# Node-graph layer on one core: two tiles of x ahead of the node types, and the type scan in steps of the key pass

## What is computed

```python
xn = layernorm(x)                                     # per node, no gain
# 1. graph attention: per-type projections of xn, one softmax per edge type over all its edges
K, Q, V = (type_proj(xn, node_type, W, b) for W, b in (Wk, bk), (Wq, bq), (Wv, bv))
scores = sum((K[src] @ Wa[t]) * Q[dst]) / sqrt(32) * relation_pri[t]
agg = segment_sum(softmax(scores over edges of type t) * (V[src] @ Wm[t]), dst)
gnn = layernorm(agg + xn) * ln_g + ln_b
# 2. linear attention over all nodes
q, k, v = split(xn @ Wqkv.T);  q, k = elu(q) + 1, elu(k) + 1
kv, ksum = sum_s k[s] (x) v[s], sum_s k[s]            # a sum over all nodes
t = (q @ kv) / (q . ksum + 1e-6)
x1 = layernorm(t + xn) * g1 + b1;  mix = layernorm(mlp(x1) + x1) * g2 + b2
x = x + gnn + mix
# 3. feed-forward on the top half of the nodes by a routing weight, added to x
```

## Time and profile before

| | us |
|---|---|
| median of 3 runs | 1085.01 |
| lowest, highest | 1084.25, 1085.23 |
| profiled execution, its own time | 1085.92 |
| its span (first to last instruction) | 1083.9 |
| granted PE clock, mean over the span | 0.898 of full speed |

### The profile page before, as it was taken

One profiled execution on the slowest core, in us unless ns is written; L12 is line 12 of the kernel. 1 busy time (PEld: TensorE's weight loads), 2 busy tenths in 40 slices (PEclk: granted clock), 3 DMA queues, 4 the chain that ended last, 5 costly groups with the idle time before them and its releaser, 6 DMA issues. The chain is left out here.

```text
span 1083.9 us, 18408 instructions
## 1 busy us (share of the span) xinstructions
PE 911.0 (84%) x5317; PEld 652.2 (60%) x5317; DVE 803.5 (74%) x1700; ACT 589.0 (54%) x1532; POOL 637.6 (59%) x820
## 2 busy tenths in 40 slices
PE   4989999999848778778777878787769939999997
PEld 3776777777524444444444444444439828888886
DVE  6754788787648878888888888888858938885541
ACT  2655999988336666666666666666641203332121
POOL 4614777777577777777777777777720037662000
PEclk9999999999967888888888888888888969999999
DMA  9822343334477777787877777877717232210020
GB/s 284 245 77 89 124 167 134 142 137 139 166 238 231 239 238 235 238 235 237 236 238 240 235 236 237 236 236 239 228 57 255 86 106 79 59 35 5 1 97 22
DMA packets 96936, 183.09 MB, mean 169 GB/s; under 512 B 15845, under 2 KB 65580, under 8 KB 96836
## 3 DMA queue, kind: packets, MB, share of 16 engines
q0 software_dynamic: 38896, 129.86, 38.7%
q1 hardware_dynamic: 54660, 48.76, 14.9%
q10 hardware_dynamic: 3280, 3.28, 0.9%
HBM read 147.79 MB, written 34.06 MB: 168 GB/s over the span
## 5 line engine op out<-in xcount | busy, mean ns | idle before, releaser
L1356 POOL DMA_INDIRECT big<-kv_scratch,src_i x336 | 318.6, 948 | 102.3 <-issue 100.8
L1518 PE MATMUL ps<-edge 64*128 64x256 f32 x784 | 146.6, 505 | 4.1 <-DMA edge<-q_scratch 4.0
L1637 DVE TENSOR_TENSOR big<-big,ps 128x1024 f32<-128x1024 f32 x84 | 102.3, 1218 | 54.1 <-DMA big<-kv_scratch,src_i 53.9
L1534 PE MATMUL ps<-big,edge 128*64 128x256 f32 x672 | 116.7, 478 | 25.8 <-DVE big L1696 14.3
L1518 PEld LDWEIGHTS ps<-edge 64*128 64x128 f32 x784 | 86.7, 239 | 48.1 <-issue 34.6
L1421 ACT ACTIVATE edge<-edge 128x64 f32<-128x64 f32 x392 | 102.9, 334 | 0.0
L1644 DVE TENSOR_REDUCE ps<-big 128x32 f32<-128x1024 f32 x84 | 102.4, 1219 | 0.1
L1696 DVE TENSOR_TENSOR big<-big,ps 128x1024 f32<-128x1024 f32 x84 | 99.0, 1212 | 0.0
L1534 PEld LDWEIGHTS ps<-big,edge 128*64 128x64 f32 x672 | 53.1, 166 | 71.3 <-DVE big L1696 34.6
L2095 PE MATMUL ps<-big 128*128 128x256 f32 (+1 forms) x416 | 92.0, 377 | 2.2 <-ACT big L2013 2.2
L2026 ACT ACTIVATE big<-ps,fb 128x256 f32<-128x256 f32 (+1 forms) x104 | 39.5, 463 | 94.4 <-PE ps L2095 94.4
(11 more groups left out here) (346 smaller groups left out, 1965.3 us busy)
## 6 DMA issues: line engine op xcount, KB each, us to landing
edge<-q_scratch SPq DMA_DIRECT2D x196, 64.0 KB
big<-kv_scratch,src_i POOLq DMA_INDIRECT x336, 3.9
agg_scratch<-big SPq DMA_DIRECT2D x16, 252.0 KB
xn_scratch<-big ACTq DMA_DIRECT2D x5, 640.0 KB, 5.2
mix_scratch<-big SPq DMA_DIRECT2D x25, 128.0 KB, 1.7
edge<-mix_scratch SPq DMA_DIRECT2D x1, 3200.0 KB, 13.3
big<-xn_scratch SPq DMA_DIRECT2D x25, 128.0 KB, 2.6
edge<-in_x SPq DMA_DIRECT2D x24, 128.0 KB, 2.3
```

The costliest lines, as they stand in the source:

```text
L1356: pool.indirect_dma_start(kv_slots[s][:, k, :], None, kv_d[0:N, :], bass.IndirectOffsetOnAxis(ap=src_i[:, e:e + 1], axis=0)).then_inc(got[ ...
L1518: ins = pe.matmul(qr_ps[g % 2][:, (2 * hg + k) * D:(2 * hg + k + 1) * D], ohT[64 * hg:64 * hg + 64, g % 2, k * P:(k + 1) * P], qwin[64 * h ...
L1534: ins = pe.matmul(sums_of(g)[64 * hg:64 * hg + 64, :], oneh[:, s, k, hg * 64:hg * 64 + 64], kv_slots[s][:, 2 * hg + k, D:2 * D], start=(k ...
L1637: dve.tensor_tensor(k_rows, k_rows, qr_ps[g % 2].rearrange("p (k d) -> p k d", d=D), ALU.mult).then_inc(pr, 1)
```

## The change

Nothing is computed differently. The order and the place of steps in the prologue change:

- SP issues x tiles 0 and 1 and the key weights first, without waiting for a clearing; then types and the rest of x. The last x tile waits for a second clearing.
- POOL clears the types' tile first, makes the constants, and clears the raw edge tile and the last x row behind them. Its inverse deviations of parts 0 and 1 stand between the constants.
- There are six parts instead of four: tiles 0-1, 2-4, 5-9, 10-14, 15-19, 20-24.
- DVE takes statistics of tiles 0 and 1 first, then casts and marks the types, normalises tiles 0 and 1, takes the statistics of tiles 2 to 4, copies the type sums, and enters the key pass. The scan stands behind kf of tile 4, the first tiles behind 5, the positions behind 6. Most other attached steps move back by three tiles, and slots, window marks, type marks and outside stand behind 17, 18, 19 and 20.
- PE's edge turns stand behind keys 9, 13 and 15 instead of 6, 10 and 12, the bases behind 11 instead of 8. The permutation stays behind 15.
- POOL's marks: four, then the deviations of part 4, ten, those of part 5, eleven.

The diff, cut to its core:

```diff
-        PARTS, BY_DVE = (0, 5, 10, 15, NT), 10
+        PARTS, BY_DVE = (0, 2, 5, 10, 15, 20, NT), 10
...
             def _(sp):
+                qkv = a["mix_WqkvT"].rearrange("(c p) o -> p c o", p=P)
+                sp.dma_start(rows[:, 0:2, :], x_d[0:2 * P, :].rearrange("(t p) d -> p t d", p=P)).then_inc(s_x0, 16)
+                sp.dma_start(wkvT, qkv[:, :, D:3 * D]).then_inc(s_wkv, 16)
                 sp.wait_ge(s_clear, 1)
...
                 for j in range(5):
-                    n = 5 if j < 4 else 4
...
+                    first, end = max(2, 5 * j), min(5 * j + 5, NT - 1)
+                    sp.dma_start(rows[:, first:end, :],
+                                 x_d[first * P:end * P, :].rearrange("(t p) d -> p t d", p=P)).then_inc(s_xc[j], 16)
+                sp.wait_ge(s_clear, 2)
                 sp.dma_start(rows[0:LAST, NT - 1, :], x_d[(NT - 1) * P:N, :]).then_inc(s_x, 16)
...
             def _(pool):
                 c = Chain(pool, pc)
-                pool.memset(raw[:, 0:2, ERAW - 1, :], 0)
-                pool.memset(raw[:, 2, ERAW - 1, :], ETY)
-                pool.memset(typ_i[:, :], NTY)
-                pool.memset(rows[:, NT - 1, :], 0.0).then_inc(s_clear, 1)
+                pool.memset(typ_i[:, :], NTY).then_inc(s_clear, 1)
...
+                pool.tensor_copy(iota_p, iota_pi).then_inc(s_const, 1)
+                pool.memset(raw[:, 0:2, ERAW - 1, :], 0)
+                pool.memset(raw[:, 2, ERAW - 1, :], ETY)
+                pool.memset(rows[:, NT - 1, :], 0.0).then_inc(s_clear, 1)
...
+                inverse_deviations(0)
                 c(pool.iota(slot_i, pattern=[[1, NS]], base=0, channel_multiplier=0))
...
+                inverse_deviations(1)
...
-                inverse_deviations(0)
+                inverse_deviations(2)
+                inverse_deviations(3)
                 pool.wait_ge(s_pos, 1)
-                mark_slots(0)
-                mark_slots(1)
-                inverse_deviations(1)
-                for t in range(2, 8):
+                for t in range(0, 4):
                     mark_slots(t)
-                inverse_deviations(2)
-                for t in range(8, 14):
+                inverse_deviations(4)
+                for t in range(4, 14):
                     mark_slots(t)
-                inverse_deviations(3)
+                inverse_deviations(5)
...
-                    if t == 6:
+                    if t == 9:
                         turn_edges(1, 0)
-                    if t == 8:
+                    if t == 11:
                         pe.wait_ge(s_edge, 1)
...
-                    if t == 10:
+                    if t == 13:
                         turn_edges(2, 2)
-                    if t == 12:
+                    if t == 15:
                         turn_edges(0, 3)
...
                 statistics(0)
-                step, at = 1, 0
-                while step < NT:
...
+                dve.wait_ge(s_types, 32)
+                dve.wait_ge(s_const, 1)
+                dve.tensor_copy(typ_t[0:NT, :], typ_i[0:NT, :]).then_inc(s_tyf, 1)
...
+                front(0)
+                statistics(1)
+                dve.wait_ge(s_tysum, 1)
...
-                front(0)
-                first_tiles()
-                positions()
                 for t in range(NT):
...
                     if t == 0:
-                        statistics(1)
+                        front(1)
+                    if t == 1:
+                        statistics(2)
                     if t == 2:
-                        front(1)
+                        statistics(3)
                     if t == 3:
-                        statistics(2)
+                        front(2)
                     if t == 4:
+                        scan_types()
+                    if t == 5:
+                        first_tiles()
+                    if t == 6:
+                        positions()
+                    if t == 7:
+                        statistics(4)
+                    if t == 8:
                         dve.wait_ge(s_edges, 16 * 9)
...
-                    if t == 5:
-                        statistics(3)
-                    if t == 6:
-                        slot_types()
-                    if t == 8:
+                    if t == 9:
                         mark_tiles()
-                    if t == 7:
+                    if t == 10:
                         dve.wait_ge(s_eT, 1)
...
                         dve.wait_ge(s_edge, 1)
-                    if t == 9:
+                        slot_types()
+                    if t == 11:
+                        statistics(5)
+                    if t == 12:
                         bases()
-                    if t == 10:
+                    if t == 13:
                         distances()
-                    if t == 11:
+                    if t == 14:
...
-                    if t == 12:
+                    if t == 15:
                         beyond()
-                    if t == 13:
+                    if t == 16:
...
-                    if t == 14:
-                        window_marks(c, dve, rel, inw)
-                    if t == 16:
-                        type_marks(c, dve, inw, rel)
                     if t == 17:
                         slots()
                     if t == 18:
+                        window_marks(c, dve, rel, inw)
+                    if t == 19:
+                        type_marks(c, dve, inw, rel)
+                    if t == 20:
                         outside()
```

More of the change, by code:

```diff
@@ L413, in build @@
             "edges_in", "types_in", "x_in", "weights_in", "mix_q_weights_in", "blocks_in", "vectors_in"))
-        s_xc = [sem(f"x_in{j}") for j in range(5)]
+        s_x0, s_xc = sem("x_first_in"), [sem(f"x_in{j}") for j in range(5)]
         s_xnst, s_padst = sem("xn_stored"), sem("padding_stored")
@@ L546, in _, with inverse_deviations @@
                 c(pool.iota(iota_pi, pattern=[[0, 1]], base=0, channel_multiplier=1))
+                pool.tensor_copy(iota_p, iota_pi).then_inc(s_const, 1)
+                pool.memset(raw[:, 0:2, ERAW - 1, :], 0)
+                pool.memset(raw[:, 2, ERAW - 1, :], ETY)
+                pool.memset(rows[:, NT - 1, :], 0.0).then_inc(s_clear, 1)
+                def inverse_deviations(part):
+                    first, end = PARTS[part], PARTS[part + 1]
+                    pool.wait_ge(s_var, part + 1)
+                    c(pool.tensor_scalar(var_all[:, first:end], mv_all[:, first:end, 1], EPS_LN, None, ALU.add))
+                    r = rstd_all[:, first:end]
+                    if first < BY_DVE:
+                        pool.tensor_tensor(r, var_all[:, first:end], nhalf[:, first:end], ALU.pow).then_inc(s_rstd, 1)
+                        return
+                    c(pool.tensor_tensor(r, var_all[:, first:end], nhalf[:, first:end], ALU.pow))
+                    c(pool.tensor_tensor(nmr_all[:, first:end], mv_all[:, first:end, 0], r, ALU.mult))
+                    pool.tensor_scalar(nmr_all[:, first:end], nmr_all[:, first:end], -1.0, None, ALU.mult).then_inc(s_rstd, 1)
+                inverse_deviations(0)
                 c(pool.iota(slot_i, pattern=[[1, NS]], base=0, channel_multiplier=0))
@@ L990, in _ @@
                 dve.memset(bd_m[:, :, :], 0.0).then_inc(s_bdz, 1)
-                dve.wait_ge(s_types, 32)
-                dve.wait_ge(s_const, 1)
-                dve.tensor_copy(typ_t[0:NT, :], typ_i[0:NT, :]).then_inc(s_tyf, 1)
-                dve.wait_ge(s_tyT, 1)
-                for y in range(NTY):
-                    ins = dve.tensor_scalar(is_ty[:, y, :], ps[7][:, 0:NT], float(y), None, ALU.is_equal)
-                ins.then_inc(s_isty, 1)
-                dve.wait_ge(s_tysum, 1)
-                v3 = "p (y t) -> p y t"
-                dve.tensor_copy(before_ty, ps[7][:, 0:NTY * NT].rearrange(v3, y=NTY))
-                dve.tensor_copy(total_ty, ps[7][:, 256:256 + NTY * NT].rearrange(v3, y=NTY))
-                c(dve.tensor_copy(scan[0], ps[7][:, 256:256 + NTY * NT].rearrange(v3, y=NTY)))
                 def statistics(part):
@@ L1007, in statistics @@
                     for t in range(first, end):
-                        if t % 5 == 0:
+                        if t == 0:
+                            dve.wait_ge(s_x0, 16)
+                        elif t == 2 or t % 5 == 0:
                             dve.wait_ge(s_xc[t // 5], 16)
@@ L1024, in _, with scan_types @@
                 statistics(0)
-                step, at = 1, 0
-                while step < NT:
-                    dve.tensor_copy(scan[1 - at][:, :, 0:step], scan[at][:, :, 0:step])
-                    c(dve.tensor_tensor(scan[1 - at][:, :, step:NT], scan[at][:, :, step:NT], scan[at][:, :, 0:NT - step],
-                                        ALU.add))
-                    step, at = 2 * step, 1 - at
+                dve.wait_ge(s_types, 32)
+                dve.wait_ge(s_const, 1)
```

(19 more changed lines are left out.)

19 lines of the change are left out of this document (2 added, 17 removed).

## The result

The changed kernel takes 1089.93 us (median of 6 runs, 1088.64 to 1090.93) against 1084.66 (6 runs) for the kernel before on the same chip: a ratio of 1.005, 95% interval 1.004 to 1.006. It is **slower by 5.3 us**, or 0.5%. The profiled execution has a span of 1087.6 us and a time of 1089.69; the span of before was 1083.9.

A forecast was written before the change was run, and what follows sets the result against it. From about 78 us all hangs on the key pass's end, so the prologue counts at full price; lead −6.6, tiles 0 to 11 +3.9, marks +4.5, tiles 16 to 24 +0.7, clock +2.0: +4.5, 1089.5 us (8 in 10: 1084.0 to 1093.5).

The forecast's parts named there:

- Head: Start of the prologue: first join at about 13.0 to 13.5 us, a lead of 6.6 us (bounds 5.5 and 7).
- Rival D: Head: types land behind the weights at 8 us or later, lead 4 or less: 1092 to 1094 us; chance 0.04.
- Tiles 0 to 11: Early key pass: DVE's steps take 32.9 us, leaving 2.7 of the 6.6 us lead; +3.9 us.
- Part 5: Clock in the prologue: the two longest PE stands priced at 0.8 and 1.2 us; bounds 0 to about 4.5.
- Marks: GpSimd's lane marks end at 56.1 us, PE waits 3.4 ahead of the permutation; +4.5 us up to tile 16.
- Tiles 16 to 24: Late key pass, four adjoining DVE steps: 18.5 us where it was 17.8; +0.7 us.
- Clock: The prologue's clock term: PE falls to the lower clock behind its longest stands; +2.0 us.
- The signs: Prologue trace: first key turn near 9 us, positions ready at 32 to 35, PE idle ahead of the permutation at 55 to 58.
- A: Key pass: moved work all hidden in DVE's idle time, marks in time: −5.9, 1079.1 us; chance 0.09.
- B: Permutation: marks in time but pace lost: −0.9 to +0.5, about 1084.5 us; chance 0.15.
- C: Key pass: every stand drops the clock, one in step 13 to 20 as well: +8, 1093 us; chance 0.09.
- The shared port: GpSimd's marks beside two-input VectorE instructions: all 25 at the slower value would end about 0.4 us later.

The follow-up runs named there:

- e1: Changed kernel with the permutation behind key tile 18 instead of 15, and DVE's late steps reordered (slots behind 20): 1083.97 us against 1084.26 for the kernel before.
- e10: Changed kernel with only the permutation moved, behind key tile 17 instead of 15: 1198.37 us against 1197.79 for the kernel before on that slower chip.
- e11: Changed kernel run again unaltered, on a slower chip: 1204.07 us against 1197.79 for the kernel before there.
- e9: Changed kernel with only the permutation moved, behind key tile 16 instead of 15: 1200.67 us against 1197.79 for the kernel before on that slower chip.
- e5: Kernel before with eight of GpSimd's lane marks made a second time, nothing moved: 1197.67 us against 1197.16 for the kernel before on that slower chip.
- e6: Kernel before with twenty of GpSimd's lane marks made a second time, nothing moved: 1207.91 us against 1197.16 for the kernel before on that slower chip.
- e3: Changed kernel with eight extra, never-read matmuls while PE waits for the marks: 1090.10 us against 1084.26 for the kernel before.
- e4: Changed kernel with scan and tiles 2 to 4 ahead of the pass, other steps rearranged, permutation behind tile 16: 1078.38 us against 1084.26 for the kernel before.
- e7: Changed kernel with tiles 2 to 4 normalised ahead of the first key join: 1200.19 us against 1197.16 for the kernel before on that slower chip.
- e8: Changed kernel with normalisation of tiles 5 to 9 and statistics of 10 to 14 exchanged: 1199.56 us against 1197.16 for the kernel before on that slower chip.
- e2: Changed kernel's head alone, with scan, first tiles and positions ahead of the pass as in the kernel before: 1085.35 us against 1084.26 for the kernel before.

## Why the prediction was right

The forecast was 1089.5 us, 4.5 over the median of before; measured are 1089.93, and 5.3 over the kernel before of the same chip. The mechanism forecast for each part is in the trace: the lead at tile 0, its loss in steps that were full, the late marks, PE standing for them, and the clock falling behind that. That the number is so close is in part luck, as the steps show:

- **Head.** The first turn at 8.47 (forecast 8.8 to 9.3), the first join at 12.64 (13.0 to 13.5), a lead of 7.0 (6.6, bounds 5.5 and 7). The two tiles of x were in use at 3.48, sooner than the 4.2 to 4.9 that I took from the five-tile transfers. The types, issued behind the weights, were cast at 5.8, as taken (5.9). Rival D falls.
- **Tiles 0 to 11.** Forecast 32.9 us, measured 35.6 (12.64 to 48.27). Of the misfit of 2.7, 2.2 lie in two steps. Step 0 took 4.11 and not 3.1: its matmuls ran at the slow pace (1.91 us at 13.93 where I put 1.03), although the profile writes a granted clock of 1.00 there. Step 3 took 5.10 and not 3.9, because the clock fell at 24.0 in the middle of it. Part 5 had 0.8 for the second and nothing for the first. The other ten steps were right to 0.4 us each. So 0.3 us of lead was left in this pair of traces, not 2.7. Part of this is chance: in e1, e10 and e11, the same program up to there, the group behind the turn of tile 2 took 1.03 and step 0 took 3.0 us, as forecast. Over all six such traces, tiles 0 to 11 took 34.4 to 35.7 us, which is 0.7 to 2.0 above the forecast with its 0.8 for the clock.
- **Marks.** Released at 35.27 (32.8), ended at 57.31 (56.1), a stand of 2.68 (3.4, bounds 2 to 5). Two misses offset each other. PE asked 2.1 us later than I had put it, since the pass was behind by 2.4. The last part's deviations also came 2.5 later (48.44, forecast 45.9), but from there the marks took 8.9 us and not 10.2. The clock fell behind the stand. From tile 12 to 16 it took 14.95, against 14.3 + 1.2 for the clock. This is the step that decides the sign, and e1, e9 and e10 show it: with the permutation two or three tiles later, and nothing else gained, the 5 to 6 us are gone. e5 and e6 show the cover that was there before.
- **Tiles 16 to 24.** 18.68 (18.5), with stands of 0.92 and 1.51 us at the long steps (2.8 forecast in all).
- **Clock.** Two falls in the pass, behind the stand at tile 5 and behind the marks, as taken. The Trainium skill, page "TensorE: Matmul & The Clock Gate", section "Why this matters for your kernels", advises against idle gaps between bursts. The traces agree for the gap at the marks: with 2.65 us or more of it the granted clock fell to 0.5 in five traces of five, and in e3, where the gap was filled, it stayed at 1.00. What the forecast did not ask is how the execution that it measured from had fared. The trace of before had falls at 20.3 and at 78.3; e5, in the same order, had none. There the pass ended 1.2 us earlier, and the opening of the next stage was 1.6 us shorter.
- **The sum.** At the last key tile the terms were forecast at +4.5 and came to +5.8. The lead was 0.4 better, tiles 0 to 11 cost 6.7 and not 3.9 + 0.8, the marks 5.2 and not 4.5 + 1.2, and tiles 16 to 24 cost 0.9 and not 0.7. Behind the pass 1.6 came back that the forecast had not, and the span was 3.7 longer. The medians, whose scatter is not read from any trace, differ by 5.3, and against the 1085.01 from which the forecast started the measured 1089.93 is 4.9 more. That this came within 0.5 us is better than the terms deserve.
- **The signs.** Three lay just outside their bounds: the first join at 12.64 (13 to 13.5), the marks' release at 35.27 (32 to 35) and the last join at 81.90 (79 to 81). The decisive one, PE idle ahead of the permutation at 55 to 58 with GpSimd's last mark as releaser, was met.
- **The rivals.** A, all hidden in DVE's idle time, was refuted as put, but e4 shows that it was a matter of places: with the scan and tiles 2 to 4 in the one long wait that DVE has left, 9.87 to 12.64, and the steps behind in another order, the whole lead is kept. B needed the marks in time, which e1 and e10 make so: 1083.97 in e1, where B had put 1084.5. C, more falls of the clock, did not come: there were two in the pass.
- **The shared port.** The prediction drew here on the Trainium skill, page "SBUF — State Buffer", section "Who interferes with whom", for marks beside operations with two inputs in SBUF. The ten marks of 41.29 took 0.584 each and the eleven of 50.75 0.596, so they were not slowed this time; the last step of the tile marks with two such inputs had ended at 41.20. In e4, where the tile marks lie beside them again, the fifteen marks from 38.83 to 49.08 took 0.683 each. One step of the deviations, at 40.47 beside the tile marks, took 0.84 us instead of 0.27. The slowing is there in both, but no run separates it from other causes, and it is too small to decide anything here.

## What to carry to other kernels

A result that an engine off the path makes has a cover that can be measured: its end against the moment at which the path asks for it. Before the input of such a step is moved later, put that cover (7.9 us here) beside the shift of the result's end (11.0 us here, from an input that came 16 us later), on every engine that takes the input and not only on the one that makes it. If the shift is longer, move the place at which the path asks as well: here two tiles were enough (e10). And look for the wait in which the moved work would lie free: a better place for the scan was the 2.8 us ahead of the first tile, not a step of the pass that already exceeded a tile's 1.95 us. Last, before a step is priced by one trace, see how far two traces of the same program lie apart: here 2.2 us at tile 12.

## What the runs showed of the hardware

- A stand of PE can cost more than its length, and not always the same. The table has the stretches with a granted clock near 0.5, read in windows of 0.25 us from 6 to 91 us, and the longest stands of PE ahead of or inside them, with the times at which the stands ended.

| trace | stands, ended at | granted clock near 0.5 |
|---|---|---|
| before | 2.00 at 20.09; 0.60 and 0.75 up to 78.49 | 20.25 to 24.0; 78.25 to 82.0 |
| e5 | 1.29 at 20.07 | none |
| e6 | 1.85 at 20.07; 6.05 at 60.38 | 20.75 to 24.25; 58.25 to 65.25 |
| changed | 2.31 at 22.87; 2.68 at 57.37 | 24.0 to 27.75; 58.25 to 61.75 |
| e11, the same kernel | 2.67 at 21.65; 2.68 at 56.85 | 22.0 to 25.5; 56.0 to 63.0 |
| e9 | 2.32 at 22.08; 0.58 at 56.57 | 23.0 to 26.75 |
| e3 | 2.32 at 24.23; 0.60 and 0.75 up to 83.87 | 84.5 to 88.0 |
| e1 | 2.67 at 20.80 | 21.0 to 24.5 |
| e10 | 2.66 at 20.75 | 21.5 to 25.0 |
| e7 | 2.62 at 19.83; 2.66 at 55.07 | 20.0 to 23.5; 54.0 to 61.0 |
| e8 | 2.65 at 54.71 | 56.0 to 59.5 |
| e2 | 4.31 at 18.15; 0.59 and 0.75 up to 77.75 | 17.25 to 24.25; 78.75 to 82.25 |
| e4 | 1.20 at 12.86 | none |

- Stands of 2.00 and 2.31 us were followed by a fall and one of 2.32 (e3) was not, so these traces give no length of a stand that decides. The same kernel paid 3.5 us at the low level behind its stand at the marks in one execution and 7.0 in another.
- In the head, PE's groups ran at about half pace although the profile writes a granted clock of 1.00 for 8 to 20 us: four matmuls of 128x256 took 1.91 us at 13.93 in the changed kernel and 1.03 at 14.05 in e11. There the durations, and not the granted clock, tell the pace.
- A stand that was filled with matmuls left the clock high there (e3).
- 256 KB of x, issued as the first transfer at 0.81, were in use 3.48 us after the start of the span; the types, issued behind 768 KB at 1.81, at 5.8 us.
